# A gated cross-attention and decoder layer on one core: probabilities turned by DMA instead of TensorE, softmax pieces by pairs of heads, and another order between the two attentions

## The reference, cut to what matters

```python
q, k = rms_norm(layernorm(x)), rms_norm(ctx)     # 16 heads of 16; 4 key heads of 16; rotary on both
attn = softmax(where(causal, q @ k.T * scale, -1e30))
x = x + tanh(g_xattn) * ((attn @ v).reshape(4, 256, 256) @ w_out.T)
h = layernorm(x)
a = layernorm(h) * ln1_w + ln1_b                 # 16 heads of 128
q, k, v = a @ wq + bq, a @ wk + bk, a @ wv + bv  # rotary on q and k
probs = softmax(where(causal, q @ k.T / sqrt(128), min))
h = h + (probs @ v) @ wo + bo
out = x + tanh(g_ffn) * (h + moe(layernorm(h)))  # top 2 of 4 experts
```

## Time and profile before

| | |
|---|---|
| median of 3 runs | 498.89 us (496.23 to 500.24) |
| the profiled execution | 499.9 us |
| its span, first to last instruction | 498.1 us |
| mean granted TensorE clock | 0.978 |
| busy: PE, PEld, DVE, ACT, POOL | 441.2, 375.2, 382.8, 239.6, 233.5 us |
| stages by the span | setup to 31, cross-attention to 121, between to about 169, steps 4 to 57 of the self-attention to 409, the rest of it and norms to 450, experts to 498 |

### The profile page before, as it was taken

One profiled execution on the slowest core, in us unless ns is written; L12 is line 12 of the kernel. 1 busy time (PEld: TensorE's weight loads), 2 busy tenths in 40 slices (PEclk: granted clock), 3 DMA queues, 4 the chain that ended last, 5 costly groups with the idle time before them and its releaser, 6 DMA issues.

```text
span 498.1 us, 10649 instructions
## 1 busy us (share of the span) xinstructions
PE 441.2 (89%) x3342; PEld 375.2 (75%) x3358; DVE 382.8 (77%) x1190; ACT 239.6 (48%) x613; POOL 233.5 (47%) x319
## 2 busy tenths in 40 slices
PE   0289998898777899999999999999999999678994
PEld 0156676575665799999999999999999998567884
DVE  5876669776366877787787887778777787885997
ACT  2035655453112554645655556555655547455451
POOL 5945809710236626635645445446356331233642
PEclk9999999999779999999999999999999999979999
DMA  8100000200024333253253342352342340000011
GB/s 285 35 1 3 2 1 3 86 1 1 6 46 98 82 112 83 65 149 82 49 143 84 80 123 76 79 147 63 84 131 58 85 109 20 1 1 0 2 44 42
DMA packets 20145, 31.93 MB, mean 64 GB/s; under 512 B 6160, under 2 KB 8336, under 8 KB 20112
## 3 DMA queue, kind: packets, MB, share of 16 engines
q1 hardware_dynamic: 16192, 22.83, 18.4%
q10 hardware_dynamic: 3920, 8.69, 5.8%
HBM read 13.68 MB, written 1.05 MB: 30 GB/s over the span
## 4 chain that ended last, share of the span: by engine, by line
PE 68%; DVE 24%; issue 4%; POOL 1%; DMA 1%; ACT 1%; SPq 0%; DVEq 0%; POOLq 0%
PE bank L1199 35%; PE bank L1279 5%; PE bank L1242 5%; PE bank L1270 4%; DVE yacc L1034 3%; PE bank L1241 3%; PE bank L1280 3%; PE bank L1152 2%; DVE yacc L1043 2%; PE bank L1119 2%; DVE nxm L813 2%; PE bank L1137 2%; PE bank L1097 1%; PE bank L1135 1%; DVE small L646 1%
## 5 line engine op out<-in xcount | busy, mean ns | idle before, releaser
L404 POOL TENSOR_TENSOR room<-room,qk_room 128x512 f32<-128x512 f32 x64 | 82.4, 1287 | 107.1 <-DMA qk_room<-qk_room 107.0
L545 ACT ACTIVATE probs<-sm,nm 128x128 f32<-128x128 f32 (+1 forms) x128 | 57.4, 450 | 115.5 <-DVE nm L920 115.5
L1199 PE MATMUL bank<-hH,qk_parts 128*128 128x512 f32 x256 | 82.2, 403 | 0.0
L843 DVE SCALAR_TENSOR_TENSOR qk_room<-bank,qk_bias,cst_sb 128x512 f32<-128x512 f32 x64 | 48.0, 750 | 37.6 <-PE bank L1199 36.2
L1199 PE MATMUL bank<-hL,qk_parts 128*128 128x512 f32 x128 | 63.1, 493 | 6.5 <-DVE room L843 5.7
L1199 PEld LDWEIGHTS bank<-hH,qk_parts 128*128 128x128 f32 x256 | 49.6, 194 | 10.2
L843 DVE SCALAR_TENSOR_TENSOR room<-bank,qk_bias,cst_sb 128x512 f32<-128x512 f32 x64 | 47.6, 744 | 0.0
L1199 PE MATMUL bank<-woH,o_parts 128*128 128x256 f32 x256 | 46.5, 280 | 0.0
L813 DVE TENSOR_REDUCE nxm<-bank 128x2 bf16<-128x512 f32 (+1 forms) x48 | 32.6, 688 | 12.4 <-PE bank L1120 11.8
L503 ACT ACTIVATE probs<-bank 128x512 f32<-128x512 f32 x48 | 28.5, 596 | 25.7 <-PE bank L1137 25.0
L1199 PE MATMUL bank<-woL,o_parts 128*128 128x256 f32 x128 | 38.5, 301 | 1.1 <-DVE o_parts L908 1.1
(11 more groups left out here) (198 smaller groups left out, 1230.4 us busy)
## 6 DMA issues: line engine op xcount, KB each, us to landing
qk_room<-qk_room SPq DMA_DIRECT2D x128, 128.0 KB, 2.3
stg<-in_wqkv ACTq DMA_DIRECT2D x6, 768.0 KB, 4.6
stge<-in_we ACTq DMA_DIRECT2D x7, 256.0 KB, 3.3
stg<-in_wqkv SPq DMA_DIRECT2D x2, 768.0 KB, 6.2
stgo<-in_wo ACTq DMA_DIRECT2D x6, 256.0 KB, 3.6
x_sb<-in_x SPq DMA_DIRECT2D x4, 256.0 KB, 6.1
out_y<-yacc SPq DMA_DIRECT2D x4, 256.0 KB, 2.1
cst_sb<-in_cst SPq DMA_DIRECT2D x1, 520.0 KB, 7.0
```

Source lines behind the costliest of these rows:

```text
L404: pool.tensor_tensor(v, v, qk_sw[:, q, :], ALU.subtract).then_inc(s["rope_done"], 1)
L545: ins = act.activation(PR[:, q, a:e], sm[:, q, a:e], ACT.Exp, bias=nm[:, q, t:t + 1], scale=-1.0, accum_out=rs[:, q, t:t + 1])
L843: return dve.scalar_tensor_tensor(out.rearrange("p (b t) -> p b t", b=2), O_B[q][:, :].rearrange("p (b t) -> p b t", b=2), qk_bias[:, c:c ...
L1199: ins = pe.matmul(outp, l, r, start=(m == 0), stop=(m == n - 1))
```

## The change

**Probabilities turned by DMA.** TensorE's three transposes and ACT's copy out of bank 2 go. Instead POOL splits each unit's probabilities into 16-bit halves (`split`, 768 elements per partition), SP issues one transposing DMA (`dma_start_transpose`, six blocks of 128 x 128 of 2 bytes), and ACT joins the halves again in SBUF (768 elements per partition). The lag of the values goes from 2 steps to 4, that of the output projection from 4 to 6, and the drain has 6 steps instead of 4; the values alternate between banks 2 and 3. SP's and POOL's steps are written out instead of looped. `rope_cos` moves ahead of the normalization on DVE.

**Cross-attention.** The pieces z = 1 and 2 are now pairs of heads over both key tiles, so that a piece needs only its own maxima; `x_values` runs once for three pieces (12 matmuls); the exponentials have six slots.

**Between the attentions.** Chunks 0 to 3 go to banks 0 to 3 (`project_first`); chunk 0 is placed inside the last pieces, chunk 1 in two halves around `out_turn(3)`; the first scores come ahead of `norm_turn(3)`. On DVE and ACT the last outputs come before the hidden state of batch 2; `residual` makes the row for the turn (`nh`) before `yacc`; both rotary chunks 0 and 1 come before the residual of batch 3; the last hidden state is split in two halves, of which DVE makes the second low part.

**End.** `while_exp` and `extra` are two units later.

```diff
-        probs = sb("probs", [P, 4, 512])
+        probs = sb("probs", [P, 6, 512])
+        halves = sb("halves", [P, 2, 2, 384], U16)
+        turned = sb("turned", [P, 4, 6, P], U16)
...
+        def unrolled_steps(step):
+            for T in range(NU + 6):
+                step(*divmod(T, U))
...
 # SP, in step T, behind swap(T + 6)
+                if unit(i, j, 1):
+                    sp.wait_ge(s["b_split"], U * i + j)
+                    if unit(i, j, 5):
+                        sp.wait_ge(s["b_merge"], U * i + j - 4)
+                    sp.dma_start_transpose(turned[:, (j - 1) % 4, :, :], halves[:, 1 - j % 2, :, :].rearrange("p h n -> p (h n)")).then_inc(s[f"d_pt{1 - j % 2}"], 16)
...
 # POOL, in step T, between low_qk and rope_add
+            def split(i, j):
+                pool.wait_ge(s["b_norm"], U * i + j + 1)
+                if unit(i, j, 2):
+                    pool.wait_ge(s[f"d_pt{j % 2}"], 16 * (4 * i + j // 2))
+                pool.tensor_copy(halves[:, j % 2, :, :], PR[:, j % 2, 0:384].bitcast(U16).rearrange("p (n h) -> p h n", h=2)).then_inc(s["b_split"], 1)
...
 # ACT, in step T, ahead of the exponentials of T
+                if unit(i, j, 3):
+                    act.wait_ge(s[f"d_pt{1 - q}"], 16 * (4 * i + (j - 3) // 2 + 1))
+                    if unit(i, j, 5):
+                        act.wait_ge(s["b_pv"], T - 4)
+                    act.activation(PTs[:, 1 - q, 0:384].bitcast(U16).rearrange("p (n h) -> p h n", h=2),
+                                   turned[:, (j - 3) % 4, :, :].rearrange("p (h c) n -> p h (c n)", h=2), ACT.Copy).then_inc(s["b_merge"], 1)
...
-                if unit(i, j, 1):
-                    act.wait_ge(s["b_pt"], T)
...
-                    act.activation(PTs[:, 1 - q, 0:384], bank[2][:, 0:384], ACT.Copy).then_inc(s["b_ptcopy"], 1)
...
 # TensorE, in step T
-                if unit(i, j, 1):
-                    pe.wait_ge(s["b_norm"], T)
...
-                    for n in range(3):
-                        ins = pe.transpose(bank[2][:, n * P:(n + 1) * P], PR[:, 1 - q, n * P:(n + 1) * P], ident)
-                    ins.then_inc(s["b_pt"], 1)
-                if unit(i, j, 2):
...
+                if unit(i, j, 4):
...
+                    pe.wait_ge(s["b_merge"], T - 3)
...
+                    pe.matmul(value_bank(j)[:, 0:256], V[:, 2 * b, r * HD:(r + 1) * HD], PTs[:, q, 0:256], start=True, stop=False)
...
 # TensorE, x_turned, z = 1 and 2
+                    by_keys = PT_B[p % 2][:, :].rearrange("p (k h n) -> p k h n", k=2, h=2)
...
+                    for kt in range(2):
+                        pe.matmul(by_keys[:, kt, :, :], kT[:, b, g, kt * P:(kt + 1) * P],
+                                  qT[:, h // 8, 1, h % 8 + first:h % 8 + first + 2, :], start=(kt == 0), stop=False)
+                    pe.matmul(by_keys[:, 1, :, :], mask_bf, ident_bf.unsqueeze(1).to_broadcast([P, 2, P]), start=False, stop=False)
+                    for n in range(2):
+                        ins = pe.matmul(by_keys[:, :, n, :], nxm[:, m % 3, 4 + first + n:5 + first + n].to_broadcast([P, P]),
+                                        ident_bf.unsqueeze(1).to_broadcast([P, 2, P]), start=False, stop=(n == 1))
...
 # TensorE, in the last pieces and behind them
+                if p == NPX + TLAG - 1:
...
+                    project_first(0)
...
+            norm_turn(B - 2)
+            pe.wait_ge(s["s_max"], NPX)
+            o_turn(NPX // 3 - 1)
+            project_first(1, (0,))
+            out_turn(B - 1)
+            project_first(1, (1,))
+            out_project(B - 1)
+            pe.wait_ge(s["s_exp"], NPX)
+            project_first(2)
+            pe.wait_ge(s["wv_ready"], 1)
+            pe.wait_ge(s["m6_free"], len(M6))
+            project_v(0, 0, False)
+            project_v(1, 1, True)
+            scores(0, 0)
+            norm_turn(B - 1)
+            project_first(3)
             pe.wait_ge(s["h_ready"], 3)
             project_v(2, 2, True)
...
 # DVE, behind the pieces
-            residual(B - 1, 0)
-            residual(B - 1, 1)
             rope(0)
-            for phase in (2, 3, 4, 5):
+            rope(1)
+            for phase in range(6):
                 residual(B - 1, phase)
-            rope(1)
-            hidden_t(B - 1)
...
+            while_exp = {63: [(0, 0)], 64: [(0, 1), (0, 2)], 65: [(0, 3)]}
+            extra = {65: [(0, 4), (0, 5)],
+                     66: [(1, 0), (1, 1)], 67: [(0, -1), (1, 2), (1, 3), (1, 4), (1, 5)], 68: [(1, -1)]}
```

More of the change, by code:

```diff
@@ L428, in step @@
                     low_qk(j, i + 1)
-                if j == 3 and not (isinstance(i, int) and (i == 0 or i >= NP - 1)):
+                if unit(i, j, 0):
+                    split(i, j)
+                if j == 5 and not (isinstance(i, int) and (i == 0 or i >= NP - 1)):
                     low_o(i)
@@ L942, in step @@
                         dve.wait_ge(s["wqk_bias"], 4 * (i + 1) + j - 2 + 1)
[L943 removed]
+                    rope_sin(T + LEAD, q, c, O_B[q], True)
+                    rope_cos(O_B[q], c, groups[g])
                 last = isinstance(i, int) and i == NP
[L945 removed]
+                if unit(i, j, 4) and last:
                     o_low(i, j)
@@ L964, in step @@
                     dve.tensor_scalar(PR[:, q, P:3 * P], PR[:, q, P:3 * P], rs[:, q, 1:2], None, ALU.mult).then_inc(s["b_norm"], 1)
-                if unit(i, j, -LEAD):
-                    rope_cos(q, c, groups[g])
-                if unit(i, j, 2) and not last:
+                if unit(i, j, 4) and not last:
                     o_low(i, j)
```

243 lines of the change are left out of this document (127 added, 116 removed).

## The result

The changed kernel takes 479.65 us (median of 4 runs, 478.29 to 480.98) against 498.74 of the kernel before on the same chip: a ratio of 0.9622, 95% interval 0.9574 to 0.9670, so 19.1 us less. 467 was forecast, 31.7 less.

A forecast was written before the change was run, and what follows sets the result against it. PE was taken to bound the steps and nearly the cross-attention. -17.8 - 6 - 10 - 1 + 2.5 = -32.3 took the profiled 499.9 us to 467.6, as a median 467; range 455 to 488 for 8 in 10.

The forecast's parts named there:

- Term 1: Steps 4 to 57: three transposes leave PE, 0.33 us a step; -17.8 us, ends -18 and -12.
- Term 2: Cross-attention: new pieces and joint values save PE time; -6 us, ends -7.4 and 0 if DVE's bursts set the pace.
- Term 3: Between the attentions: the new order starts chunk 4 earlier, about 139 against 149.2; -10 us, ends -7 and -13.
- Term 4: Steps 0 to 3: PE's waits for normalizations go, rotary and DVE set the pace; -1 us, ends 0 and -2.
- Term 5: The end: longer path from last normalization to last o_low delays all that follows; +2.5 us, ends 0 and +5.
- The chain that I priced at 7.0 us: At the end, last normalization to o_low(63): split, transfer, join, values, oH and handovers; 7.0 us instead of 4.5.
- B: Steps 4 to 57: the DMA transfer is the bound and the kernel gets slower, 569 us at packet prices; chance 0.15.
- C: Steps 4 to 57: DVE takes PE's place, the step stays at 4.44 us, 484 us in all; chance 0.18.

The follow-up runs named there:

- run 3: Changed kernel with POOL's conversion of the low output weights ahead of the split of the same step; 477.2 us, ratio 0.955.
- run 1: Changed kernel with the old cross-attention score pieces, values of one piece at a time and four exponential slots; 485.6 us, ratio 0.971.
- run 8: Changed kernel with the old order between the attentions, the new pieces, values and DMA turns kept; 484.8 us, ratio 0.971.
- run 12: Changed kernel with low_o first, reordered ramp, two-step lag and gradual catch-up at the end, plus POOL's weights and yacc later in cross-attention; 465.7 us, ratio 0.931.
- run 10: The changed kernel measured once more, unaltered; 481.46 us, ratio 0.9638.
- run 2: Changed kernel with the old steps: transposes on TensorE, old lags and last steps; cross-attention and order between the attentions as changed; 489.3 us, ratio 0.981.
- run 6: Changed kernel with DVE's addition first at the end, low output weights ahead of the split, units 62 and 63 turned on TensorE; 477.3 us, ratio 0.958.
- run 4: Changed kernel with DVE's addition of an output pair ahead of the second norm's pieces in the last steps; 480.5 us, ratio 0.964.
- run 9: Changed kernel with low_o first and reordered ramp, plus units 58 to 63 turned on TensorE, values catching up in step 60; 471.0 us, ratio 0.945.
- run 11: Changed kernel with low_o first, reordered ramp, units 58 to 63 on TensorE, values catching up over steps 60 and 61; 470.5 us, ratio 0.941.
- run 7: Changed kernel with POOL starting the value and output weights only after DVE has packed the last q; 482.0 us, ratio 0.966.

## Why the prediction was right in sign and 12.7 us off in size

**What bounds it.** Right. PE sets the steps, and the pairs in the chain are 8.27 us apart (8.2 forecast).

**Term 1, steps 4 to 57: -17.8 forecast, -13.1 measured.** The mechanism was right, the size off in three ways. A step lost 0.311 us, not 0.33: the transposes' distance was read at one place, and PE has 4.133 without them; -16.8 instead of -17.8 over 54. One step in eight waits on POOL's low output weights, which the new `split` had pushed behind itself: 6 x 0.38 = 2.3 us, shown by run 3. I had named `rope_add` as what stands behind `split` and had not gone through the other operations that it moves. And from the scores of unit 4 to those of unit 7 it takes 13.8 us, through the wait for the value weights, where three steps of 4.13 would be 12.4: 1.4 us. The prices: split 0.82 (0.90), join 1.08 (0.94), landing 2.8 (3.5, and 3 to 4 named as the sign; three in eight land after 3.7 to 5.9), engine time 1.2 us a unit (1.5), DVE 3.55 a step (3.6). None of them sets the step.

**Term 2, the cross-attention: -6 forecast, between -2.7 and -3.9 measured.** This is the mis-sized term. Run 1 against the changed kernel gives 3.9. Run 8 against the kernel before, both with the old order behind the pieces, gives 91.8 - 90.2 = 1.6, and 2.7 when the 1.1 of low clock in run 8 is taken off; what the two comparisons differ by I have not placed. PE's waits for the maxima went from 2.4 (before) and 3.4 (run 1) to 5.0 us: the pieces now come faster than DVE's bursts let their maxima follow. With run 1 beside it, 3.9 and 1.6 make 5.5 of the 7.4 that I had counted for PE alone; since these waits are anything from 5.0 to 7.3 us in the five executions of the same code, that sum is no more than a sign. I had that as the end "0 if DVE's bursts do" and took -6 by the busy shares, 94% against 73%. A share over 90 us does not say what a burst of 3 us does with two score banks. Run 12 takes the burst beside POOL away, which gives 2.85 us more. That is not the new pieces' own gain, for the copies met POOL in the kernel before as well, and the old pieces with POOL's later work were not run. What is seen in the whole is less still, -0.7, because chunk 0 is now inside (1.45 by its matmuls, 1.0 by run 8, which has it outside: 91.1 against 90.2, both with low clock), and because about 1.1 of low clock lay behind this stretch before.

**Term 3, between: -10 forecast, -11.3 measured.** Right in size, wrong in what it is made of. The milestones fit: `nh` is turned 13.3 us behind the last values (13.3 forecast), and chunk 4 starts 16.6 behind them (17.8). But the new order is worth 6.2 us of it (run 8). The other 5.1 are there at the old order too, where PE had a clock of 1.00 and 0.85 instead of 0.71 and 0.79: by these rows some 3.5 us at the lower level instead of 13.6. At the price in the pieces (1.1 us for the 3.4 us at the lower level that 0.86 from 91 to 103 means) that difference of 10 us would be worth 3.3, an estimate, so not all of the 5.1 need be the clock. It is also one execution of each, and run 10 shows that the low clock changes its place by itself, so the 5.1 is not shown to come from the change. I had charged reduced clock to my estimate of the new order and not asked where the low clock of before would go.

**Term 4, steps 0 to 3: -1 forecast, -1.3 measured** (chunk 4 to the scores of unit 4: 19.9 and 18.6 us). The number is right, partly by luck: with the old steps and the new order (run 2) the same stretch takes 21.4 us (136.11 to 157.55). So the change of the steps gave 2.8 us there, and the rest of the change took 1.5 back, which I had not foreseen.

**Term 5, the end: +2.5 forecast, +6.5 measured.** The step that failed is the sentence "The two extra steps themselves hold no work". The chain that I priced at 7.0 us took 8.9 (402.96 + 0.35 to 412.24; 10.2 in runs 3, 8 and 10, whose ends are no longer), but run 6 takes the transfer out of it, and beside run 4 the chain stays at 8.4 and the end moves by 0.5. Those two steps hold values, `o_low` and additions, and the addition 28 comes two steps later: the norm of batch 0, whose pieces lay beside the last exponentials, now lies behind them. From the last normalization to the last addition it takes 16.1 us instead of 11.8. Undoing the lag for the last units alone (runs 9 and 11) gave 2.3 and 3.6 of the 4 us that I had missed; undoing all of it (run 2) 5.6.

**The rivals.** B, the transfer as bound: no. A unit takes 1.2 us of the engines, under the 3.1 from which B decides, and PE waits for no join in the steps. The Trainium skill, "VectorE: DVE Perf Modes", section "The three transpose paths", has 1309 ns for one block; the estimate of 7.9 us a unit made of it is far from this transfer, which does six blocks in one DMA and lands after 2.8. The estimate of 0.75 us from the 261 GB/s in the Trainium skill, "DMA: Bandwidth & Descriptors", section "Latency and other measured facts", is nearer to the 1.2 and too low. C, DVE takes PE's place: not in the steps (4.13 each). From 150 to 165 DVE is busy 14.1 of 15 us and PE 10.9, which no term had.

**The sum.** 467.6 + 4.7 (term 1) + 5.3 (the pieces, -0.7 instead of -6) + 4.0 (term 5) - 1.6 (terms 3 and 4) = 480.0, the time of the profiled execution.

## What to carry to other kernels

When an operation is added to an in-order queue, go through everything that it pushes back, once for each step of the loop, and look at the steps in which something rare stands there. A longer lag costs more at the end of a loop than its chain: list what lay beside the last units and now lies behind them. And where an engine feeds another through two buffers, compare bursts, not busy shares: ask what the consumer does in its longest stretch without a result.

## What the hardware showed that I had not expected

- The low clock of TensorE moves. Five executions of one and the same code up to unit 7 had it in different places: in three of them behind the wait of 2.3 us at 96.90, which the other two passed at full clock, and in three behind the value weights (in run 4 PE stood 3.7 us there, and the clock was 0.79 from 162 to 170; in the other two it had stood 3.5). It is the level of 1.2 GHz: a matmul of 256 columns lies 0.12 us behind the one before it at full clock and 0.21 at the lower one. It costs 1.1 us in the pieces; in the stretch to unit 7 the executions differ by 2.7, of which at most 1.7 is the clock. Runs 9 and 11, with one and the same code there, differ by 2.2 in the pieces (92.2 and 89.9). So two profiles of kernels that do the same can differ by 2 to 3 us in one stretch. Single profiles are to be compared stretch by stretch, with the clock beside them.
- DVE operations of two or four elements a partition (0.16 us) took 1.1 to 1.3 us beside a two-input operation of POOL, three times in the kernel after and five times in run 7. In a chain of a dozen such operations one of these costs as much as seven others.
- Three 128x128 blocks of 4 bytes, split into six blocks of 2, are turned by one DMA in 2.8 us to landing, at 1.2 us of the engines' time, in 51200 additional packets for 64 of them. By packets at the price of the old queue (90.5 ns each) it would have been 4.35; the additional packets cost 23 ns of an engine each.
